# A selected LSTM after a graph propagation: the low part of h column by column, and the first block's weights in 2 KB rows

## What is computed

```python
def step(carry, x_t):
    h, c = carry
    sel_in = jnp.concatenate([h, c, x_t], axis=-1)
    logits = sel_in @ W_sel.T + b_sel
    onehot = jax.nn.one_hot(jnp.argmax(logits, axis=-1), Sx)
    g_all = einsum(x_t, W_ih) + einsum(h, W_hh) + b_ih + b_hh   # all four sets
    g = jnp.einsum('bsg,bs->bg', g_all, onehot)
    i, f, g, o = jnp.split(g, 4, axis=-1)
    c2 = sigmoid(f) * c + sigmoid(i) * tanh(g)
    h2 = sigmoid(o) * tanh(c2)
    return (h2, c2), h2
```

## Time and profile before

| | us |
|---|---|
| median of 3 runs | 6864.05 (6862.68 to 6869.19) |
| the profiled execution's own time | 6865.91 |
| its span, first to last instruction | 6864.2 |
| first and last `hsum` (L837) | 1446.2 and 6835.6 |

### The profile page before, as it was taken

The page is one execution under the profiler, slowest core; times in us unless marked ns, Lnnn a source line. Parts: engine busy times, 40 slices in busy tenths (PEclk is TensorE's granted clock), DMA queues, the critical chain, the costliest instruction groups (busy, mean ns, idle before and its releaser), DMA issues.

```text
span 6864.2 us, 340774 instructions
## 1 busy us (share of the span) xinstructions
PE 6126.8 (89%) x126674; PEld 4106.7 (60%) x126675; DVE 3617.9 (53%) x19152; ACT 1804.5 (26%) x6561; POOL 1685.8 (25%) x4128
## 2 busy tenths in 40 slices
PE   6727999679999999999999999999999999999986
PEld 3423444566666666666666666666666666666664
DVE  5453111235555556555665555566556665565555
ACT  1001000412233233222332332233333333233321
POOL 5732111412222222222222222222222222222220
PEclk8758999579999999999999999999999999999999
DMA  3220000522222122222222222222222222222210
GB/s 94 1 77 0 0 0 0 177 70 60 60 61 61 57 61 62 58 60 61 64 63 61 62 61 61 60 62 64 61 61 63 64 63 61 60 63 61 61 52 27
DMA packets 715589, 389.97 MB, mean 57 GB/s; under 512 B 47835, under 2 KB 703579, under 8 KB 715296
## 3 DMA queue, kind: packets, MB, share of 16 engines
q1 hardware_dynamic: 684322, 369.66, 18.4%
q0 software_dynamic: 24192, 0.10, 1.1%
q10 hardware_dynamic: 7038, 19.69, 0.9%
HBM read 370.96 MB, written 18.38 MB: 57 GB/s over the span
## 4 chain that ended last, share of the span: by engine, by line
PE 70%; issue 6%; DVE 6%; DMA 0%; DVEq 0%; SPq 0%; POOL 0%; ACT 0%; POOLq 0%
PE ps L1007 33%; PE ps L1069 15%; PE ps L1016 8%; PE ps L1000 5%; PE ps L996 4%; DVE hsum L837 2%; PE ps L993 2%; PE ps L983 2%; DVE osum L845 1%; DVE acts L855 1%; DVE gates L842 1%; DVE osum L848 1%; DVE cprod L851 0%; PE ps L972 0%; DMA wring<-in_w_ih 0%
## 5 line engine op out<-in xcount | busy, mean ns | idle before, releaser
L1007 PE MATMUL ps<-WH,hparts 128*2 128x384 f16 x49760 | 2297.3, 326 | 194.4 <-issue 173.2
L837 DVE TRANSPOSE_TENSOR_REDUCE hsum<-ps 128x12 f32<-128x384 f32 x1250 | 728.8, 583 | 1784.5 <-PE ps L1007 1774.2
L1007 PEld LDWEIGHTS ps<-WH,hparts 128*2 128x2 f16 x49760 | 1042.4, 83 | 1046.7 <-issue 297.0
L1069 PE MATMUL ps<-xcur,wcur 128*128 128x64 f32 x9728 | 1342.8, 281 | 89.1 <-issue 15.1
L1069 PEld LDWEIGHTS ps<-xcur,wcur 128*128 128x128 f32 x9728 | 1179.3, 191 | 276.6 <-issue 213.6
L449 POOL COPY xT<-hfull 128x4 f32 x1250 | 239.5, 192 | 3721.7 <-DVE hfull L866 3721.7
L465 POOL COPY wcur<-wring 128x512 f32<-128x512 f32 x1216 | 743.4, 611 | 449.7 <-ACT gxb L593 447.8
L1016 PEld LDWEIGHTS ps<-WH,hparts 128*2 128x2 f16 x40000 | 596.7, 83 | 359.0 <-issue 316.6
L1016 PE MATMUL ps<-WH,hparts 128*2 128x128 f16 x40000 | 775.4, 219 | 8.6
L578 ACT ACTIVATE gx_now<-gxb 128x16 f32 x1250 | 269.7, 216 | 1832.6 <-DVE pick L831 1709.3
L963 PE MATMUL ps<-O,Adj 128*128 128x512 f16 x3000 | 650.3, 380 | 77.2 <-DVEq L743 77.2
(11 more groups left out here) (147 smaller groups left out, 5001.8 us busy)
## 6 DMA issues: line engine op xcount, KB each, us to landing
wring<-in_w_ih SPq DMA_DIRECT2D x1280, 256.0 KB, 2.9
gxb<-in_w_hh ACTq DMA_DIRECT2D x32, 512.0 KB, 4.0
adjacency<-Adj SPq DMA_DIRECT2D x2, 6400.5 KB, 24.7
Adj<-adjacency SPq DMA_DIRECT2D x10, 640.0 KB, 7.3
sim<-adjacency SPq DMA_DIRECT2D x10, 640.0 KB, 6.5
adjacency<-total,where_ POOLq DMA_INDIRECT x168
x_rows<-X SPq DMA_DIRECT2D x1, 2560.0 KB, 8.7
wring<-x_rows SPq DMA_DIRECT2D x10, 256.0 KB, 3.6
```

The source lines that it names most:

```text
L837: dve.tensor_reduce(hsum[:, :], gate_ps.rearrange("p (c q) -> p c q", q=32), AX.X, ALU.add, apply_transpose=True).then_inc(turned, 1)
L1007: last = nc.tensor.matmul(gate_ps[32 * j:32 * j + 2, :], hparts[:, k, :], WH[:, s * KC + k, part, j, 0:3 * P], start=(k == 0 and part == 0 ...
L1069: last = nc.tensor.matmul(unit_ps, wcur[:, k, :], xcur[:, k, :], start=(k == 0), stop=(k == KC - 1))
```

## The change

Two edits.

**The low part of h.** `hfull` moves behind the low part. The low part is no longer hfull - high on 128 x 4, but four instructions on 128 x 1, tanc[:, k] * osig[:, k] - high[:, k], with the column of `osig` as the per-partition scalar operand. Each signals its own semaphore `h_ready[k]`, and TensorE's guessed cell products wait for column k's ahead of column k.

**The first block's weights.** A piece of the ring holds one k for all four units instead of one unit for all k: one row of 2 KB per partition. TensorE goes through k outermost and accumulates in four banks at once; a piece is freed by the last product that reads it, and TensorE waits for its own products once in a group. The loads of the later blocks stay as they are.

```diff
-        h_ready = sem("h_ready")
+        h_ready = [sem(f"h_ready{k}") for k in range(SUB)]
...
-                    for u in range(SUB):
-                        sp.wait_ge(wring_free, sp.snap(q * (G * SUB) + (g * SUB + u + 1)))
-                        load_unit(q, g, u)
+                    for k in range(KC):
+                        sp.wait_ge(wring_free, sp.snap(q * (G * KC) + (g * KC + k + 1)))
+                        sp.dma_start(wring[:, k, :, :].rearrange("p u n -> p (u n)"),
+                                     w_ih[:, bass.ds(q, 1), order[g], k * D:(k + 1) * D].rearrange("p a n -> p (a n)")
+                                     ).then_inc(wring_in[k], 16)
...
-            dve.memset(hparts[:, :, :], 0.0).then_inc(h_ready, 1)
+            link(dve.memset(hparts[:, :, :], 0.0))
+            for k in range(SUB):
+                dve.sem_inc(h_ready[k], 1)
...
-                dve.tensor_tensor(hfull[:, :], osig[:, :], tanc[:, :], ALU.mult).then_inc(h_full, 1)
                 dve.tensor_tensor(hparts[:, :, 0], osig[:, :], tanc[:, :], ALU.mult).then_inc(h_high, 1)
                 dve.wait_ge(h_high, m)
-                dve.tensor_tensor(hparts[:, :, 1], hfull[:, :], hparts[:, :, 0], ALU.subtract).then_inc(h_ready, 1)
+                for k in range(SUB):
+                    dve.scalar_tensor_tensor(out=hparts[:, k, 1:2], in0=tanc[:, k:k + 1], scalar=osig[:, k:k + 1], in1=hparts[:, k, 0:1],
+                                             op0=ALU.mult, op1=ALU.subtract).then_inc(h_ready[k], 1)
+                dve.tensor_tensor(hfull[:, :], osig[:, :], tanc[:, :], ALU.mult).then_inc(h_full, 1)
...
-                for u in range(SUB):
-                    pe.wait_ge(wring_in[u], pe.snap(q * 16 + 16))
-                    pe.sem_inc(pieces_seen, 1)
-                    pe.wait_ge(proj_out, pe.snap(q * SUB + (u + 1)))
-                    for k in range(KC):
-                        last = nc.tensor.matmul(ps[:, 4 + u, 0:TB], wring[:, u, k, :], xT[:, k, 0:TB], start=(k == 0), stop=(k == KC - 1))
-                    last.then_inc(proj_mm, 1)
-                    pe.wait_ge(proj_mm, pe.snap(q * SUB + (u + 1)))
-                    pe.sem_inc(wring_free, 1)
+                for k in range(KC):
+                    for u in range(SUB):
+                        if u == 0:
+                            pe.wait_ge(wring_in[k], pe.snap(q * 16 + 16))
+                            pe.sem_inc(pieces_seen, 1)
+                        if k == 0:
+                            pe.wait_ge(proj_out, pe.snap(q * SUB + (u + 1)))
+                        last = nc.tensor.matmul(ps[:, 4 + u, 0:TB], wring[:, k, u, :], xT[:, k, 0:TB], start=(k == 0), stop=(k == KC - 1))
+                        if k == KC - 1:
+                            last.then_inc(proj_mm, 1)
+                        elif u == SUB - 1:
+                            last.then_inc(wring_free, 1)
+                pe.wait_ge(proj_mm, pe.snap(q * SUB + SUB))
+                pe.sem_inc(wring_free, 1)
...
-            def cell_products(s, done):
+            def cell_products(s, done, n=None):
                 for k in range(KC):
+                    if n is not None:
+                        pe.wait_ge(h_ready[k], n)
...
                     logits(n)
-                    pe.wait_ge(h_ready, n)
-                    cell_products(s, guess_mm)
+                    cell_products(s, guess_mm, n)
```

## The result

| | before | after |
|---|---|---|
| median, us (4 runs each, side by side) | 6866.62 (6862.68 to 6872.74) | 7079.6 (7074.7 to 7082.56) |
| ratio | | 1.0309, 95% interval 1.0291 to 1.0326 |
| the profiled execution's own time | 6865.91 | 7079.38 |
| its span | 6864.2 | 7077.6 |
| first and last `hsum` | 1446.2 and 6835.6 | 1409.9 and 7048.3 |

The kernel is 213 us slower. The table's last line splits that already: the first step comes 36.3 us earlier and the stretch of the steps is 249.1 us longer (5638.4 against 5389.3).

A forecast was written before the change was run, and what follows sets the result against it. The 1,250 recurrence steps bound the kernel, with the pick path only 0.06 us behind the cell path. Right guesses +165, repeated steps +73 and projection -33 make +205 us, giving 7070 us, range 6930 to 7125.

The forecast's parts named there:

- Their spacing, 0.13: VectorE's queue behind tanh(c): the four low-part instructions start 0.13 us apart, 0.07 plus 0.06 for the column scalar.
- From `lmax` to `hsum`, 1.41: Pick path in a step: where the pick comes last, the next `hsum` starts 1.41 us after `lmax`.
- The threshold of 2.36: Right-guess step: the pick sets its length once `lmax` starts later than 2.36 us after `hsum`.
- Right guesses: 945 steps whose guess is settled at once: about 0.17 us longer each, +161 to 170 us.
- Repeated ones: 305 steps that repeat their products behind `pick`: they take the 0.24 us delay in full, +73 us.
- The cell path's gain: Guessed cell products on TensorE: they can start 0.04 us earlier, worth nothing once the pick is last.
- The load of the next guess: TensorE, behind the wait for the last low part: 0.31 us long, over before `pick` ends with 0.1 to spare.
- Projection: First block's projection on TensorE: groups of 8.05 instead of 10.12 us, 16 groups, -33 us.
- (1): Low parts: the column as scalar is free, starts 0.07 us apart, `lmax` as now; 6796 us, chance 0.09.
- (2): Low parts: the instructions do not overlap, starts 0.21 us apart; 7465 us, chance 0.03.
- (3): First block's projection gets TensorE's high clock, saving 93 us instead of 33; 7010 us, chance 0.07.
- (4): First block's weight ring is late, so the projection gains 13 us or nothing; 7083 to 7103 us, chance 0.05.

The follow-up runs named there:

- the pads: Projection edit alone, plus unused 128x1 instructions behind the single low part: one with a column scalar 6831.96 us, three 7003.93, three with a constant 6853.81.
- columns of constants: Changed kernel, but hfull stays ahead of the high part and the four low parts are hfull column minus high column, without osig's scalar: 6860.89 us.
- three constant pads: Kernel before with the projection edit, plus three unused 128x1 instructions with constant 0.5 as scalar behind its one low part: 6853.81 us.

## Why the prediction was right

Forecast 7070 (6930 to 7125), measured 7079.6. The steps of it, in their order:

- *The low parts' start.* Low 0 starts 1.96 after `hsum` in the median step, 1.95 forecast. From the high part to it is 0.201, where 0.20 was taken.
- *Their spacing, 0.13.* Measured 0.131. The bounds of 0.07 and 0.21 both fall away: a column costs what was taken for it, and no instruction waits for the one ahead to end (each is 0.219 long and the next starts after 0.131). Both terms hold: 0.07 with a constant (0.070 in the pads, but for one interval of 0.098) and 0.06 for the column, read from instructions on 128x512.
- *`lmax`* at 2.558, forecast 2.55; `pick` ends at 3.13, forecast 3.12.
- *From `lmax` to `hsum`, 1.41*: 1.405 (median period of 3.963 less 2.558). The threshold of 2.36 that follows from it is borne out by the pads: at 2.35 a right step pays 0.01 in the mean, at 2.50 its median is 0.129 longer (3.904 against 3.775), which puts the threshold at 2.37.
- *Right guesses*, +161 to 170 forecast: from 3.801 to 3.984 in the mean, +172.4 over 944 steps between the first `hsum` and the last. *Repeated ones*, +73: +76.7 over 305. At 2.35 the repeated steps already pay: `lmax` comes 0.064 later in them than with the projection alone, and each takes 0.056 longer with columns of constants and 0.041 with three constant pads, give or take the scatter of 0.01 to 0.02. That they take up such a small delay in full is not shown.
- *The cell path's gain*, 0.04: L1020 starts 2.234 after `hsum`, L1007 did 2.248, so 0.014. This is the one term that was well off. Low 0 started 0.01 later than summed and took about 0.22 for 0.21; TensorE started 0.052 behind its end, as it does behind the single low part, where 0.05 was taken. It changed nothing, since the gain was worth nothing.
- *The load of the next guess*, covered by 0.1: it starts 2.745 after `hsum`, where it was 2.535, so it is 0.21 later because it stands behind the wait for the last column. It ends 0.07 ahead of `pick`'s end in the median step and 0.02 at the least. Covered, by less than forecast.
- *Projection*, -33: from its first product to the end of its last 162.1 us before (1274.05 to 1436.12) and 129.3 after (1268.23 to 1397.57), -32.7, at 7.99 a group where 8.05 was forecast. The first step comes 36.3 earlier in the profiled execution, because the stage began 5.8 earlier there and 2.2 were lost between it and the first `hsum`. The -5.8 is scatter in the main: over all traces the stage begins from 1265.7 to 1272.5 in the eight kernels with rows of 2 KB and from 1269.6 to 1274.1 in the three with rows of 512 B. That the rows bring some of it is not excluded.
- *Sum.* +205 forecast, +213 measured: 249.1 instead of 238 in the steps, 36.3 instead of 33 ahead of them. The 5.8 of scatter is luck that took some of the error away.

The rivals: the column is not free (1) and not without overlap (2). The high clock in the projection (3) did not come, not even with TensorE busy 40.00 of 40 us in the two kernels without its own wait, where the granted clock stayed at 0.50, which is 1.2 GHz. The ring was hardly late (4): behind the first load TensorE waited for it twice, 2.4 us in all.

Three sums of the prediction do not come out as written. None of them touches the forecast. A spacing of 0.12 to 0.14 moves `lmax` by 0.04 either way, which over 1,250 steps is 50 us, so its range would be 7020 to 7120 and not 7035 to 7105. The ring's cover is 6.05 - 4.3 = 1.75 us, not 1.5. And a gain of only 13 in rival 4 gives 7090, not 7083.

The page that spoke against the forecast, the Trainium skill, "VectorE: DVE Perf Modes", section "The TRN2 errata", knows no extra for a column as scalar. The pads measure it as 0.06 us an instruction, so here the measurement decides; without the column the estimate from its figures, 0.06 us, stands beside 0.07.

## What to carry to other kernels

Splitting one instruction into several so that a consumer can start earlier lengthens the producer's queue by the whole sum, and whatever stands behind it there pays. So find the second path through the step and its slack before the first path is shortened: here it was 0.06 us, and it showed only in a step where that path came last. Steps that repeat their work may have no such slack, and are counted by themselves. And an engine that waits for its own result only to pass a signal on can leave that signal to the engine that waits for the result anyway.

## What was not expected of the hardware

- A [128, 1] tile as per-partition scalar costs an instruction of VectorE on 128x1 0.06 us in spacing and 0.066 us in duration (215 against 149 ns), what it cost on 128x512. By these two sizes it is an amount per instruction, not per element.
- TensorE busy without a gap for 53 and 57 us, with f32 products of 64 columns, was granted 1.2 GHz all the while, whereas in the trace of the kernel before the transposes ahead of the projection, which begin at 1227.94, were granted 2.4 GHz from 1237.10 on the earlier trace rows. The Trainium skill, "TensorE: Matmul & The Clock Gate", section "Why this matters for your kernels", asks for continuous work to get the full clock; these runs show continuous work without it. Why the one got it and the other not stays open.

The transposes in TensorE's timeline of the kernel before:

```profile
1227.94 10.12 PE L916 MATMUL ps<-ident,O 128*128 128x128 f32 x40 [18.28 <-DVE O L761]
```
